# Reordering the first loads, and the first products around them, in a quantised-weight FFN kernel

## What is computed

```python
W = weights[condition]                        # (64, 64, 64)
y = einsum('bct,bcd->bdt', x, W)
w = (unpack6(qweight) - zero_point) * scale   # (1024, 1024), 4 six-bit values in 3 int32 words
out = x + einsum('bsk,nk->bsn', y, w) + bias
```

## Time and profile before

| | us |
|---|---|
| median of 3 runs | 287.79 (287.77 to 288.94) |
| the profiled execution's own time | 287.66 |
| its span | 285.4 |
| around the span | 2.3 |
| TensorE busy | 279.1 (98%) |
| VectorE busy | 188.6 (66%) |
| GpSimd busy | 94.5 (33%) |
| ScalarE busy | 83.3 (29%) |

### The profile page before, as it was taken

The page is one execution under the profiler, slowest core; times in us unless marked ns, Lnnn a source line. Parts: engine busy times, 40 slices in busy tenths (PEclk is TensorE's granted clock), DMA queues, the critical chain, the costliest instruction groups (busy, mean ns, idle before and its releaser), DMA issues.

```text
span 285.4 us, 8520 instructions
## 1 busy us (share of the span) xinstructions
PE 279.1 (98%) x3323; PEld 233.2 (82%) x3323; DVE 188.6 (66%) x254; ACT 83.3 (29%) x170; POOL 94.5 (33%) x38
## 2 busy tenths in 40 slices
PE   7999999899999999999999999999999999999995
PEld 3988888788888888888888888888888888888885
DVE  3685999855567666865559555676667655595554
ACT  3677412531045300732017310453006320050000
POOL 0009563234440444304443344404443044430000
PEclk9999999999999999999999999999999999999999
DMA  7982463544124521445115541145214451101112
GB/s 276 401 301 80 160 226 112 193 156 155 73 83 161 200 96 69 147 157 190 73 73 181 163 152 73 73 162 198 99 73 148 157 191 73 73 37 73 73 73 73
DMA packets 20685, 39.48 MB, mean 138 GB/s; under 512 B 6850, under 2 KB 7106, under 8 KB 20674
## 3 DMA queue, kind: packets, MB, share of 16 engines
q1 hardware_dynamic: 19730, 36.96, 36.6%
q10 hardware_dynamic: 944, 2.38, 2.3%
HBM read 22.54 MB, written 16.78 MB: 138 GB/s over the span
## 4 chain that ended last, share of the span: by engine, by line
PE 92%; DVE 4%; DMA 1%; issue 1%; ACTq 1%; ACT 0%; DVEq 0%
PE o_ps L281 78%; PE y_ps L250 8%; PE y_ps L281 2%; DVE resid L505 2%; PE o_ps L250 2%; DMA q_raw<-in_L_ffn_qweight_dram 1%; PE o_ps L292 1%; PE y_ps L263 1%; PE o_ps L263 0%; DVE o_sb L514 0%; DVE o_sb L522 0%; ACT L433 0%; ACTq L140 0%; DVE y_lo L495 0%; PE y_ps L292 0%
## 5 line engine op out<-in xcount | busy, mean ns | idle before, releaser
L281 PE MATMUL o_ps<-qT,y_hi 128*128 128x512 f32 (+2 forms) x520 | 197.9, 385 | 0.0
L281 PE MATMUL o_ps<-qT,y_lo 128*128 128x512 f32 (+2 forms) x520 | 196.7, 382 | 0.0
L614 POOL TENSOR_TENSOR resid<-x_sb,bias_bc 128x1024 f32<-128x1024 f32 x32 | 93.8, 2934 | 157.3 <-DVE o_sb L522 136.9
L281 PEld LDWEIGHTS o_ps<-qT,y_hi 128*128 128x128 f32 x520 | 97.1, 188 | 19.5 <-ACT qT L427 0.2
L281 PEld LDWEIGHTS o_ps<-qT,y_lo 128*128 128x128 f32 x520 | 97.2, 188 | 18.9
L514 DVE TENSOR_TENSOR o_sb<-o_ps,scale_bc 128x512 f32<-128x512 f32 x61 | 42.2, 692 | 76.5 <-PE o_ps L281 76.0
L522 DVE TENSOR_TENSOR o_sb<-o_sb,resid 128x512 f32<-128x512 f32 x63 | 51.3, 818 | 2.1
L402 ACT ACTIVATE junk<-x_sb 128x1024 bf16<-128x1024 f32 x32 | 33.8, 1058 | 54.1 <-DMA x_sb<-in_x_dram 54.1
L505 DVE SCALAR_TENSOR_TENSOR resid<-zs_bc,ysum,resid 128x1024 f32<-128x1024 f32 x32 | 46.0, 1438 | 0.0
L495 DVE TENSOR_TENSOR y_lo<-y_ps,y_hi 128x512 fp32r<-128x512 f32 x57 | 35.1, 683 | 5.7 <-ACT y_hi L411 5.7
L420 ACT ACTIVATE ysum<-y_ps 64x2 f32<-64x2 f32 x18 | 3.0, 165 | 106.5 <-PE y_ps L292 98.0
(11 more groups left out here) (34 smaller groups left out, 58.7 us busy)
## 6 DMA issues: line engine op xcount, KB each, us to landing
x_sb<-in_x_dram SPq DMA_DIRECT2D x32, 512.0 KB, 3.3
out_dram<-o_sb SPq DMA_DIRECT2D x63, 256.0 KB, 2.1
q_raw<-in_L_ffn_qweight_dram ACTq DMA_DIRECT2D x6, 384.0 KB, 5.4
w_sb<-in_L_cond_weights_dram SPq DMA_DIRECT2D x63, 16.0 KB, 1.9
q_raw<-in_L_ffn_qweight_dram SPq DMA_DIRECT2D x2, 384.0 KB, 6.8
scale_bc<-_L_ffn_weight_scale_dram SPq DMA_DIRECT2D x1, 512.0 KB, 5.1
zs_bc<-n_weight_zero_point_dram SPq DMA_DIRECT2D x1, 512.0 KB, 5.7
bias_bc<-in_L_ffn_bias_dram SPq DMA_DIRECT2D x1, 512.0 KB, 6.5
```

The source lines that it names most:

```text
L281: last = nc.tensor.matmul(bank, part[:, slot, kt, :], qT[:, kt, col:col + width], start=(kt == 0 and part is y_hi), stop=(kt == KT - 1 and ...
L614: nc.gpsimd.tensor_tensor(resid[:, j % RING, :], x_sb[:, j % RING, :], bias_bc[:], ALU.add).then_inc(xbias_ready, 1)
```

## The change

Loads: SyncE's queue now issues the condition numbers, the four matrix halves of tiles 0 and 1 (each picked just before its own issue, where `load_w` before picked both first), then x of tile 1, blocks 6 and 7, and the rest as before. ScalarE's queue issues blocks 0 and 1, x of tile 0, and after its table load blocks 2 to 5.

TensorE: block 1 is transposed ahead of the first mix, in place of the two `keep_warm` matmuls; the first quarter of tile 0 is one pass of 256 columns with `y_hi` and one with `y_lo`; the second quarter goes to another PSUM bank (`second_quarter`, the upper half of `free_banks[1]`), so the wait on `left_copied` moves to the left half of tile 1; `sum_y` waits until the second quarter is copied out. ScalarE: block 1 is placed ahead of `high(0)`, and the row sum of tile 2 ahead of the placing of block 6. VectorE: block 4 is unpacked ahead of the copy of the first quarter.

```diff
--- before.py
+++ after.py
@@ -92,6 +92,7 @@
         y_banks.append([y_bank(0, 0), o_banks[1]])
         y_banks = [[bank.rearrange("p (t r) -> p t r", t=KT) for bank in pair] for pair in y_banks]
         sum_banks = [o_banks[0], free_banks[1]]
+        second_quarter = free_banks[1][:, 2 * P:NH]
         qt_banks = [as_bits(free_banks[0]), as_bits(o_banks[1])]
 
         last_pieces = [(o_ps[:, 1, 0:NH // 2], NH, NH // 2),
@@ -160,9 +161,8 @@
 
             def load_w(j, i):
                 t = i * RING + j
-                picked = [pick(sp, t * 2 + half) for half in range(2)]
                 for half in range(2):
-                    load_w_half(sp, j % RING, half, picked[half])
+                    load_w_half(sp, j % RING, half, pick(sp, t * 2 + half))
 
             def reload(j, i):
 
@@ -190,12 +190,11 @@
 
 
             sp.dma_start(ids[:], cond.rearrange("(a b) -> a b", a=1)).then_inc(ids_loaded, 16)
-            load_x(0, 0)
             sp.wait_ge(ids_loaded, 16)
-            load_w_half(sp, 0, 0, pick(sp, 0))
+            load_w(0, 0)
+            load_w(1, 0)
             load_x(1, 0)
-            load_w(1, 0)
-            for n in (4, 6):
+            for n in (6, 7):
                 load_q(sp, n)
             for j in range(2, RING):
                 load_x(j, 0)
@@ -337,31 +336,31 @@
             def left_half(kts):
                 return products(o_ps[:, 0, :], 0, NH, 1, kts)
 
+            def first_quarter(part):
+                return products(o_ps[:, 0, 0:2 * P], 0, 2 * P, 0, parts=(part,))
+
             pe.wait_ge(warm_ready, 1)
             keep_warm(WARMUP)
             pe.wait_ge(ident_ready, 1)
             transpose_q(0)
-            keep_warm(2)
+            transpose_q(1)
             wait_mix(0, 0)
             mix(0, y_banks[0])
-            transpose_q(1)
             transpose_q(2)
-            pe.wait_ge(qt_ready, 1)
+            pe.wait_ge(qt_ready, 2)
             pe.wait_ge(y_hi_ready, 2)
-            products(o_ps[:, 0, 0:P], 0, P, 0, parts=(y_hi,))
-            wait_linear(0, 0, 0)
-            products(o_ps[:, 0, 0:P], 0, P, 0, parts=(y_lo,))
-            pe.wait_ge(qt_ready, 2)
-            products(o_ps[:, 0, P:2 * P], P, P, 0).then_inc(o_ps_ready[0], 1)
+            first_quarter(y_hi)
+            pe.wait_ge(y_lo_ready, 2)
+            first_quarter(y_lo).then_inc(o_ps_ready[0], 1)
             transpose_q(3)
             wait_mix(1, 0)
             mix(1, y_banks[1])
             pe.wait_ge(qt_ready, 4)
-            pe.wait_ge(left_copied, 1)
-            products(o_ps[:, 0, 2 * P:NH], 2 * P, NH - 2 * P, 0).then_inc(o_ps_ready[0], 1)
+            products(second_quarter, 2 * P, NH - 2 * P, 0).then_inc(o_ps_ready[0], 1)
             transpose_q(4)
             transpose_q(5)
-            wait_linear(1, 0, 0)
+            pe.wait_ge(left_copied, 1)
+            pe.wait_ge(y_lo_ready, 4)
             left_half(range(0, KT // 2))
             transpose_q(6)
             left_half(range(KT // 2, KT)).then_inc(o_ps_ready[0], 1)
@@ -370,6 +369,7 @@
                 wait_mix(j, 0)
                 mix(j, y_banks[j - 2])
             pe.wait_ge(qt_ready, 7)
+            pe.wait_ge(scaled[0], 1)
             pe.wait_ge(xsum_ready, RING)
             for j in range(RING):
                 sum_y(j, free_banks)
@@ -429,15 +429,14 @@
 
             for n in range(2):
                 load_q(act, n)
+            act.dma_start(x_sb[:, 0, :], x_rows[0:P, :]).then_inc(x_loaded[0], 16)
             act.wait_ge(warm_ready, 1)
             nc.scalar.activation(junk[:, 1, 0:1], warm[:, 0:1], ACT.Copy)
-            act.wait_ge(ids_loaded, 16)
-            load_w_half(act, 0, 1, pick(act, 1))
-            for n in (2, 3, 5, 7):
+            for n in range(2, 6):
                 load_q(act, n)
             place_q(0)
+            place_q(1)
             high(0, 0, y_banks[0])
-            place_q(1)
             place_q(2)
             sum_x(0, 0)
             place_q(3)
@@ -445,8 +444,8 @@
             sum_x(1, 0)
             place_q(4)
             place_q(5)
+            sum_x(2, 0)
             place_q(6)
-            sum_x(2, 0)
             sum_x(3, 0)
             place_q(7)
             high(2, 0, y_banks[0])
@@ -531,13 +530,13 @@
                 unpack_q(n)
             low(0, 0, y_banks[0])
             unpack_q(3)
+            unpack_q(4)
             dve.wait_ge(o_ps_ready[0], 1)
             nc.vector.tensor_copy(o_sb[:, 0, 0:2 * P], o_ps[:, 0, 0:2 * P]).then_inc(left_copied, 1)
-            unpack_q(4)
             unpack_q(5)
             low(1, 0, y_banks[1])
             dve.wait_ge(o_ps_ready[0], 2)
-            nc.vector.tensor_copy(o_sb[:, 0, 2 * P:NH], o_ps[:, 0, 2 * P:NH]).then_inc(scaled[0], 1)
+            nc.vector.tensor_copy(o_sb[:, 0, 2 * P:NH], second_quarter).then_inc(scaled[0], 1)
             unpack_q(6)
             unpack_q(7)
             dve.wait_ge(scale_loaded, 16)
```

## The result

The change makes the kernel slower: 291.83 us (290.98 to 293.57, 4 runs) against 287.78, a ratio of 1.0148 with a 95% interval of 1.0119 to 1.0177. The profiled execution of the changed kernel is the slowest of the four, 293.57 us with a span of 291.4. Predicted were 287.2 us, and 285.8 to 288.4 as the range.

A forecast was written before the change was run, and what follows sets the result against it. TensorE, busy 279.1 of 285.4 us, was taken as the bound. Of 1.9 us of lead 0.77 get through, less 0.2 for bias: gain 0.6, profiled 287.66 to 287.1, median 287.2 us, range 285.8 to 288.4.

The forecast's parts named there:

- First mix: TensorE's start: moved half matrix issued at 4.2, landing taken as 2.3 us, so mix at 6.5 against 6.67.
- The row of 5.3: Profile row of the kernel before: a matrix took 5.3 us in this stretch; the upper landing time for the first mix.
- Rival 3: Small matrices don't overtake: first mix at 9.5 instead of 6.67, time 288.8 us; chance 0.12.
- First quarter: Tile 0's first quarter on TensorE: 256-column matmuls take 1.95 us instead of 3.61.
- ScalarE's order, block 1 first: ScalarE places blocks 0 and 1 ahead of the evacuation `high(0)`, ending at 7.8: cost 0.
- Second mix: x of tile 1, out at about 7.1, lands 4.2 to 5.4 us later; mix at 11.4 to 12.5 instead of 13.33.
- the lead: Earlier start of tile 0's first right-half matmul, at 24.46 before: about 1.9 us, or 0.8 if x of tile 1 takes 5.4.
- What takes the lead back: VectorE and GpSimd exclude each other up to `low` at 49.48; of 1.9 us of lead, 0.77 get through.
- Bias: Landing of bias on SyncE's queue: taken as 0.2 us later, bounds -0.6 and +1.2.
- The issue gap: TensorE's 0.5 us gap in the middle of the fourth mix, perhaps hidden: gain 0 to 0.5, taken 0.

The follow-up runs named there:

- the half put back: Changed kernel with the second half of tile 0's matrix back on ScalarE's queue, behind x of tile 0 and ahead of blocks 2 to 5: 287.91 us, ratio 1.001.
- the blocks held: Changed kernel with blocks 2 to 5 waiting until SyncE has issued both halves of tile 0's matrix: 289.63 us, ratio 1.0071.
- the run kept warm: Changed kernel with 18 matmuls on zeros between block 1's transpose and the first mix: 290.25 us, ratio 1.0084.
- the wide quarter: Kernel before, with only the 256-column first quarter, the second bank and ScalarE's row sum ahead of block 6: 286.97 us, ratio 0.9985.
- The probe: Changed kernel; SyncE waits for ScalarE's six blocks and x of tile 0, then issues an extra 16-row load of 1 KB rows: 294.05 us, single execution.
- the last experiment: As the wide quarter, but in the loop the first load of x of the next group waits for all four mixes: 287.32 us, ratio 0.9977.

## Why the prediction was wrong

- **First mix.** The step that failed: "nothing big stands ahead of it on its queue now, so I am near the lower end and take 2.3". The halves took 6.5 and 6.2 us, above even my upper end of 5.3. I counted what is ahead on the transfer's own queue; what counted was what both queues had issued. The row of 5.3 had no fewer bytes to wait for: as an estimate from the issues and the GB/s, 2.0 MB were still to move at 5.70 us there and 2.0 MB at 4.37 here. They moved more slowly here, 299 GB/s between 4 and 7 us against 371. I also didn't follow ScalarE's queue: I wrote down the half that leaves it, and not that blocks 2 to 5 then leave 1.4 us earlier and get in front of the matrices. That is the shown cause: with the half put back, the loss is gone, and with the blocks held, the halves land 3.5 us after their issue on the same queue. The same step had x of tile 0 "due at about 6"; it landed at 7.8, so that even with early matrices the mix could not have started at 6.5.
- **The price of the delay.** Rival 3 had the mechanism and 0.12 of the chance, at 288.8. It lacked two things: 1.3 us more of delay (10.84, not 9.5) and the clock, 0.64% or 1.8 us (the run kept warm). The two `keep_warm` matmuls that "only filled the wait" I priced at nothing under the condition that the wait stays short, and didn't price the other case.
- **First quarter.** Right. Block 3's transpose follows the first mix by 4.4 us instead of 6.1 in the three runs that show the passage at full clock (half put back 4.42, kept warm 4.41, loads of before 4.44).
- **ScalarE's order, block 1 first.** Right as to 0 at a mix of 6.5 or later. With the loads of before, block 1's transpose does hold the mix back to 7.86; the change needed block 1 early and the matrices early, and got the first only.
- **Second mix.** x of tile 1 was taken to go out at 7.1 and to land 4.2 to 5.4 us later. Three picks and issues of 1.23 us after 3.62 give 7.3, not 7.1; it went out at 7.63 and took 5.7. In the run with the half put back it took 7.2 and cost the lead 0.83 us. The same fault.
- **What takes the lead back.** The chain through GpSimd and VectorE is right where a lead existed: in the wide quarter the `low` came 0.43 us earlier, as 0.77 less bias's delay, with the first residual between GpSimd's third and fourth additions. It was so with a lead of 0.52 at the right half, less than the 0.8 from which the prediction had it. It did not matter for the changed kernel. That the wait near 50 us hangs on bias's landing is right only in part: with bias 2.8 us earlier 0.34 of it was left.
- **Bias.** Taken +0.2, measured 23.02 against 21.85, +1.2, the upper bound.
- **The issue gap.** Taken as 0 to 0.5 of gain; it was a loss of 1.0 in the profiled execution.

What has an interval below that of the kernel before is the least of the change: the 256-column quarter in its own bank with the loads of before, 0.9985, and 0.9977 with the loop's load moved. Both are gains of less than the 0.5% that one measurement can tell from nothing.

## What to carry to other kernels

At the start of a kernel, where the DMA engines are full, write down every load of all queues in one list by the time of issue, with the bytes summed up: in this kernel a load landed about when the sum ahead of it had moved, whichever queue it was on. It is a rough rule. The probe landed 0.3 MB before that point, and x of tile 0 in the changed kernel 0.6 MB after it, its own bytes counted: 1.9 MB had moved, where 1.3 were ahead or its own. Taking a wait or a small load out of a queue moves all that follows it there forward, in front of the others. And price a wait of TensorE twice, once for its length and once for the clock after it.

## What the runs showed of the hardware that was not expected

- A load of one row for each DMA engine, alone on its queue, landed 5.6 us after its issue, where the other queue had 2.9 MB issued ahead of it. The Trainium skill, "DMA: Bandwidth & Descriptors", "Issuing engines are not separate DMA queues", has the queues interleave; on this row they came close to the order of issue, and in the changed kernel SyncE's queue moved no packet from 4.2 to 7 us with a load issued at 3.14.
- Between 4 and 7 us the engines moved 371 GB/s before, and 299 in the changed kernel, 334 with the half put back, 280 with the blocks held; with x of tile 1 back at 3.6 us on SyncE's queue it was 396. The rate was low where all big loads of that stretch stood on one queue, though from 8 to 10 us the same queue alone gave over 400. Why is open.

```profile
4.00:7.00 3.00, 2.19 (x19) 1.06 (x17) 1.76 (x6) 1.39 (x2) 0.00 (x0) 1.00 0.92 299
```
```profile
4.00:7.00 3.00, 2.75 (x19) 1.55 (x17) 1.89 (x6) 0.80 (x1) 0.00 (x0) 1.00 1.03 396
```

- A single stop of TensorE of a few us brought its clock to 1.2 GHz: in the changed kernel TensorE stopped at 6.44, and the clock was 1.00 from 7 to 8 us and 0.56 from 8 to 9. It fell in the run with the blocks held as well, where TensorE had stood only from 5.5 to 7.3, and near 56 us in the changed kernel, after the gap of 1.5. The length of the stop doesn't decide it alone: with the loads of before and the new order of the work, TensorE stood for 1.65 us before 7.31, and the clock of that profile is 1.00 throughout the beginning.
- The granted clock reads 1.00 in the first microseconds too, but TensorE's pace doesn't fit it: the nine warm-up matmuls take 3.8 us, 0.42 each, where the 18 of the same shape in the run kept warm take 4.05, 0.22 each. So ahead of 5 us that reading doesn't give TensorE's pace.

```profile
1.17 3.84 PE L334 MATMUL y_ps<-warm 128*128 128x512 bf16 x9 [1.17 <-DVE warm L528]
```

- TensorE stops for 0.3 to 1.5 us in the middle of the fourth mix of the second group, waiting for nothing that the profile shows, in nearly all profiles of the study; the one with the half put back has none. It isn't the load of x that is in flight then (the last experiment); what it is stays open.
